# Relative attention takes in the norm ahead of it and the projection, norm and gate behind it

## The reference, cut to what matters

```
x = x + attn_a(layernorm(x))      # 16 heads of 16, relative positions in 63 buckets
x = x + ffn(layernorm(x))         # 16 experts, 512 tokens each, and a shared one
x = x + attn_b(layernorm(x))      # 16 heads of 64, window 128
x = x + ffn(layernorm(x))

def attn_a(x):                    # per batch b, head h
    q, k, v = split(x @ w_qkv.T); q = q * scale
    attn = q @ k.T + take(q @ rpe_k_table, idx) + take((k * scale) @ rpe_q_table, idx).T
    attn = softmax(attn)
    out = attn @ v + segment_sum(attn, buckets) @ rpe_v_table
    return heads_joined(out) @ w_proj.T + b_proj

def ffn(x):                       # its gate works on the normed rows
    scores = softmax(x @ gate_w.T)
    ...
```

## Time and profile before

| | us |
|---|---|
| median of 3 runs | 3925.07 |
| profiled execution | 3910.7 |
| its span | 3908.9 |
| first norm stage, from the span's start | 0 to 50.44 |
| relative stage's opening | 50.44 to 126.38 |
| its 32 units | 126.38 to 1156.86 |
| its last products and stores | 1156.86 to 1170.38 |
| second norm stage | 1170.38 to 1296.93 |
| the rest | 1296.93 to 3908.9 |

### The profile page before, as it was taken

How to read it: one execution, slowest core, us unless ns; L and a number is a source line. 1 busy time by engine, 2 the same in 40 slices (tenths; PEclk the granted TensorE clock), 3 DMA queues, 4 the chain that set the end, 5 groups by cost and what they waited for, 6 DMA issues and landing times. The chain is left out here.

```text
span 3908.9 us, 92834 instructions
## 1 busy us (share of the span) xinstructions
PE 3506.8 (90%) x33008; PEld 2695.1 (69%) x33008; DVE 2466.3 (63%) x5459; ACT 1826.1 (47%) x3736; POOL 1036.2 (27%) x1016
## 2 busy tenths in 40 slices
PE   3899999999986786999995999999999795999998
PEld 3566666666655675888884677667667585888887
DVE  5566666666664567676663666666666566666664
ACT  2566666666651323444442555455445432444443
POOL 0122222222220002333331343334333201232332
PEclk9999999999998897999998999999999897999999
DMA  5565666566545323443432000000000122443441
GB/s 189 151 171 167 173 174 173 167 175 175 168 129 180 115 74 126 117 119 109 116 92 82 13 20 18 21 21 18 18 21 19 59 81 100 124 113 103 127 114 32
DMA packets 372911, 407.00 MB, mean 104 GB/s; under 512 B 172689, under 2 KB 314385, under 8 KB 359057
## 3 DMA queue, kind: packets, MB, share of 16 engines
q1 hardware_dynamic: 347922, 368.09, 29.9%
q0 software_dynamic: 24576, 33.57, 4.9%
HBM read 255.49 MB, written 146.08 MB: 103 GB/s over the span
## 5 line engine op out<-in xcount | busy, mean ns | idle before, releaser
L2445 POOL TENSOR_TENSOR a_below<-a_probT,a_upper 128x512 f32<-128x512 f32 x128 | 164.3, 1283 | 724.6 <-ACT a_probT L2369 378.1
L2393 ACT ACTIVATE a_prob<-a_ps_s,a_low 128x512 f32<-128x512 f32 x512 | 319.2, 689 | 48.1 <-DVE a_low L2585 48.1
L1669 POOL TENSOR_TENSOR b_prob<-b_prob,b_rinv 128x512 f32<-128x512 f32 (+1 forms) x256 | 238.3, 935 | 386.5 <-DVE b_rinv L1730 386.3
L2254 PE MATMUL a_ps_p<-a_ident,a_prob 128*128 128x128 f32 x2048 | 309.3, 284 | 13.9 <-ACT a_band L2373 9.0
L2585 DVE TENSOR_REDUCE a_low<-a_ps_s 128x2 f32<-128x1024 f32 x256 | 313.5, 1225 | 8.8
L1607 ACT ACTIVATE b_prob<-b_score,b_low 128x256 f32<-128x256 f32 (+1 forms) x512 | 241.7, 474 | 129.6 <-DVE b_low L1725 113.8
L2254 PEld LDWEIGHTS a_ps_p<-a_ident,a_prob 128*128 128x128 f32 x2048 | 216.4, 141 | 106.1 <-issue 80.6
L2369 ACT COPY a_probT<-a_ps_p 128x512 f32<-128x512 f32 x352 | 193.9, 588 | 154.4 <-PE a_ps_p L2254 154.4
L1725 DVE CUSTOM_DVE_ANT_0 b_score<-b_ps_s,b_bias 128x256 f32<-128x256 f32 (+1 forms) x512 | 178.1, 385 | 74.9 <-PE b_ps_s L1548 71.6
L2584 DVE TENSOR_TENSOR a_ps_s<-a_ps_s,a_win 128x320 f32<-128x320 f32 (+1 forms) x256 | 135.0, 528 | 142.9 <-PE a_ps_s L2287 138.4
L903 POOL DMA_INDIRECT x<-fe_eo,fe_index_scatter x64 | 121.6, 1899 | 361.5 <-DVE fe_eo L1098 346.9
(11 more groups left out here) (426 smaller groups left out, 10402.1 us busy)
## 6 DMA issues: line engine op xcount, KB each, us to landing
a_win<-band SPq DMA_DIRECT2D x128, 384.0 KB, 4.8
prob<-a_prob SPq DMA_DIRECT2D x128, 384.0 KB, 3.6
shift<-a_gbias SPq DMA_DIRECT2D x64, 256.0 KB, 2.1
a_shifted<-shift SPq DMA_DIRECT2D x256, 64.0 KB, 2.0
a_bins<-prob SPq DMA_DIRECT2D x128, 128.0 KB, 3.5
fe_gT<-in_WgT SPq DMA_DIRECT2D x16, 1024.0 KB, 4.9
fe_uT<-in_WuT SPq DMA_DIRECT2D x16, 1024.0 KB, 5.2
fe_dT<-in_WdT SPq DMA_DIRECT2D x16, 1024.0 KB, 4.8
```

What stands on the lines that cost most here:

```text
L1669: nc.gpsimd.tensor_tensor(part, part, by_row, ALU.mult).then_inc(divided, 1)
L2254: last = nc.tensor.transpose(bank[:, c * P:(c + 1) * P], prob[:, t % 2, h, 32 + c * P:32 + (c + 1) * P], ident[:, :])
L2393: nc.scalar.activation(prob[:, t % 2, h, 32:32 + T], ps_s[pair][:, r, :], ACT.Exp, bias=low[:, h:h + 1]).then_inc(exped, 1)
L2445: nc.gpsimd.tensor_tensor(below[:, t % 2, :, :], probT[:, t % 2, :, t * P:(t + 1) * P], upper[:, :].unsqueeze(1).to_broadcast([P, HG, P]), ...
```

## The change

`norm_stage` is gone, and with it both of its uses. Its work is done inside the relative stage, for one batch at a time, in steps of the units:

- Batch b + 1, ahead: its x is loaded in round 0 (`xi`), its statistics are taken at the end of round 0, it is normalised in place in round 1 and transposed through `ps_w` (x_T) straight into `xT`. The split of x into two parts follows in the same round. For batch 0 this is done in the opening, with `ps_s` as bank.
- Batch b - 1, behind: the heads' results stay in the tile `o`, now of all 16 heads; in round 0 x is loaded again (`x1`) and GpSimd adds the bias; in round 1 heads are transposed (o_T); in round 2 they are multiplied by the projection in two halves (y), added into `x1`, and the norm is taken; in round 3 the normed rows `yn` (the same tile as `xi`) are transposed (y_T), stored both ways, and the gate's logits and softmax are made. For the last batch all of it follows after the units.

All new matmuls go through `ps_w`: LEAD and WHOLE have five new kinds, nine sections per batch. Not changed are the stages behind.

```diff
-LEAD = {"q": 3, "k": 3, "v": 2, "g_pos": 2, "g_low": 2, "g_up": 2, "s_pos": 1, "s_neg": 1, "band": 1, "bins_T": -1, "bins": -1, "out": -1}
+LEAD = {"q": 3, "k": 3, "v": 2, "g_pos": 2, "g_low": 2, "g_up": 2, "s_pos": 1, "s_neg": 1, "band": 1, "bins_T": -1, "bins": -1, "out": -1,
+        "x_T": 3, "o_T": -5, "y": -6, "y_T": -7, "logits": -7}
+WHOLE = ("q", "v", "k", "g_pos", "g_low", "g_up", "s_neg", "s_pos", "bins", "x_T", "o_T", "y", "y_T", "logits")
+ROUND_AT = {"x": 1, "in_stats": 0, "in_norm": 1, "in_pow": 0, "x_T": 1, "with_bias": 0, "o_T": 1, "y": 2, "y_stats": 2, "y_pow": 2, "y_norm": 2,
+            "y_T": 3, "logits": 3, "gate_exp": 3, "gate_end": 3}
...
-    ("max", 0), ("max", 1), ("s_pos", 0), ("probs_T", 3), ("s_neg", 0),
+    ("max", 0), ("max", 1), ("in_norm", 0), ("y", 0), ("s_pos", 0), ("probs_T", 3), ("s_neg", 0),
...
-        o = s.sb("o", [P, 2, NT, HG, AD])
+        o = s.sb("o", [P, NT, C])
+        xi = s.sb("xi", [P, NT, C])
+        x1 = s.sb("x1", [P, NT, C])
+        yn = xi
+        o_turned = s.sb("o_turned", [P, KC, T])
...
+                hold(sp, yn_out, 16 * b - 16, held)
+                hold(sp, ynT_out, 16 * b - 16, held)
+                sp.dma_start(xi[:, :, :], by_token(x_d, b)).then_inc(xi_in, 16)
+
+            def load_again(b):
+
+                hold(sp, x1_out, 16 * b + 16, held)
+                hold(sp, yn_ready, b + 1, held)
+                sp.dma_start(x1[:, :, :], by_token(x_d, b)).then_inc(x1_in, 16)
+
+            def store_x1(b):
+                hold(sp, emptied, section(b, 0, "y", 1) + 1, held)
+                sp.dma_start(by_token(x1_d, b), x1[:, :, :]).then_inc(x1_out, 16)
+
+            def store_normed(b):
+                hold(sp, yn_ready, b + 2, held)
+                sp.dma_start(by_token(xn_d, b), yn[:, :, :]).then_inc(yn_out, 16)
+
+            def store_turned(b):
+                hold(sp, emptied, section(b, 0, "y_T", 1) + 1, held)
+                sp.dma_start(by_channel(xnT_d, b), ynT[:, :, :]).then_inc(ynT_out, 16)
...
+                if has_step(b, g, "with_bias", 0):
+                    load_again(b - 1)
...
-                if g == 0 and not (isinstance(b, int) and b == B - 1):
-
-                    hold(sp, emptied, section(b, 2, "v") + 1, held)
+                if has_step(b, g, "in_stats", 0):
                     load_x(b + 1)
-                if has_step(b, g, "out", 0):
-                    store(*unit_before(b, g, 1))
+                if has_step(b, g, "y_norm", 0):
+                    store_x1(b - 1)
+                if has_step(b, g, "logits", 0):
+                    store_normed(b - 1)
                 home(b, g, 3)
+                if has_step(b, g, "logits", 0):
+                    store_turned(b - 1)
                 if has_step(b, g, "g_up", 0):
                     bias_out(*unit_after(b, g, 2), 0)
...
+            pe.wait_ge(in_normed, 1)
+            for c in range(KC):
+                for t in range(NT):
+                    last = nc.tensor.transpose(ps_s[0][:, c, t * P:(t + 1) * P], xi[:, t, c * P:(c + 1) * P], ident[:, :])
+            last.then_inc(first_turned, 1)
...
+                elif kind == "x_T":
+                    pe.wait_ge(in_normed, b + 1)
+                    for t in range(NT):
+                        last = nc.tensor.transpose(ps_w[:, t * P:(t + 1) * P], xi[:, t, k * P:(k + 1) * P], ident[:, :])
+                elif kind == "o_T":
+                    wait_copied(pe, b, NG - 1, "out", range(1))
+                    for t in range(NT):
+                        last = nc.tensor.transpose(ps_w[:, t * P:(t + 1) * P], o[:, t, k * P:(k + 1) * P], ident[:, :])
+                elif kind == "y":
+                    if b == 0 and k == 0:
+                        pe.wait_ge(late_in, 16 * 3)
+                    for t in (2 * k, 2 * k + 1):
+                        for c in range(KC):
+                            last = nc.tensor.matmul(ps_w[:, t % 2 * C:(t % 2 + 1) * C], o_turned[:, c, t * P:(t + 1) * P], proj[:, c, :],
+                                                    start=(c == 0), stop=(c == KC - 1))
+                elif kind == "y_T":
+                    pe.wait_ge(yn_ready, b + 2)
+                    for t in range(NT):
+                        last = nc.tensor.transpose(ps_w[:, t * P:(t + 1) * P], yn[:, t, k * P:(k + 1) * P], ident[:, :])
+                elif kind == "logits":
+                    for t in range(NT):
+                        for c in range(KC):
+                            last = nc.tensor.matmul(ps_w[:, t * E:(t + 1) * E], ynT[:, c, t * P:(t + 1) * P], gwT[:, c, :],
+                                                    start=(c == 0), stop=(c == KC - 1))
...
+                if kind == "x_T":
+                    last = nc.scalar.copy(xT[:, k, :], ps_w[:, :])
+                elif kind == "o_T":
+                    act.wait_ge(ynT_out, 16 * b + 16)
+                    last = nc.scalar.copy(o_turned[:, k, :], ps_w[:, :])
+                elif kind == "y_T":
+                    act.wait_ge(ynT_out, 16 * b + 16)
+                    last = nc.scalar.copy(ynT[:, k, :], ps_w[:, :])
...
+            def gate_exp(b):
+                act.wait_ge(emptied, section(b, 0, "logits") + 1)
+                nc.scalar.activation(sm[:, :, :], sm[:, :, :], ACT.Exp).then_inc(gate_exped, 1)
...
+                    if t == 3 and has_step(b, g, "in_pow", 0):
+                        power("in", b + 1)
+                    if t in (1, 2) and has_step(b, g, "with_bias", 0):
+                        with_bias(b - 1, t - 1)
+                    if t == 1 and has_step(b, g, "y_pow", 0):
+                        power("y", b - 1)
...
+            def with_bias(b, h):
+
+                hold(pool, x1_in, 16 * b + 16, held)
+                if isinstance(b, int) and b == 0 and h == 0:
+                    hold(pool, late_in, 16 * 3, held)
+                half = x1[:, 2 * h:2 * h + 2, :]
+                nc.gpsimd.tensor_tensor(half, half, bias[:, :].unsqueeze(1).to_broadcast([P, 2, C]), ALU.add).then_inc(biased, 1)
...
+            def moments_of(end, rows, b):
+                for t in range(NT):
+                    nc.vector.bn_stats(stats[end][:, t, :], rows[:, t, :]).then_inc(moments[end], 1)
+                hold(dve, moments[end], 2 * NT * b + NT, held)
+                for t in range(NT):
+                    nc.vector.bn_aggr(mv[end][:, t, :], stats[end][:, t, :]).then_inc(moments[end], 1)
+                hold(dve, moments[end], 2 * NT * b + 2 * NT, held)
+                nc.vector.tensor_scalar(var[end][:, :, :], mv[end][:, :, 1:2], LN_EPS, None, ALU.add).then_inc(var_ready[end], 1)
+
+            def normed(end, to, rows, b, ready):
+                hold(dve, rstd_ready[end], b + 1, held)
+                for t in range(NT):
+                    last = nc.vector.tensor_scalar(to[:, t, :], rows[:, t, :], mv[end][:, t, 0:1], rstd[end][:, t, :], ALU.subtract, ALU.mult)
...
+            def y_stats(b):
+                dve.wait_ge(emptied, section(b, 0, "y", 1) + 1)
+                moments_of("y", x1, b)
+
+            def y_norm(b):
+
+                hold(dve, yn_out, 16 * b + 16, held)
+                normed("y", yn, x1, b, yn_ready)
+
...
+                if kind == "y":
+                    dve.wait_ge(biased, 2 * b + k + 1)
+                    dve.wait_ge(filled, n + 1)
+                    half = x1[:, 2 * k:2 * k + 2, :]
+                    last = nc.vector.tensor_tensor(half, ps_w[:, :].rearrange("p (t c) -> p t c", c=C), half, ALU.add)
+                elif kind == "logits":
+                    logits = ps_w[:, 0:NT * E].rearrange("p (t e) -> p t e", e=E)
+                    dve.wait_ge(filled, n + 1)
+                    nc.vector.reduce_max(mx[:, :, :], logits, AX.X).then_inc(gate_step, 1)
+                    dve.wait_ge(gate_step, b + 1)
+                    last = nc.vector.tensor_tensor(sm[:, :, :], logits, mx[:, :, :].to_broadcast([P, NT, E]), ALU.subtract)
...
+            for k in range(2):
+                empty("y", B - 1, 0, ch, k)
+            y_stats(B - 1)
+            y_norm(B - 1)
+            empty("logits", B - 1, 0, ch)
+            gate_end(B - 1)
...
-        norm_stage(nc, "n0", ident, ins["x"], xnT)
-        relative_stage(nc, "a", ins, xnT, (ins["a_wT"], ins["a_wv"]), ins["a_rows"], ins["a_table"], ins["a_base"],
-                       ins["a_bins"], ins["a_bins_base"], ins["a_vbase"], trips, heads)
-        norm_stage(nc, "n1", ident, ins["x"], xnT, attn=(heads, ins["a_projT"], ins["a_bias"]), x1_d=x1, xn_d=xn, gate=ins["gateT"], scores=scores)
+        relative_stage(nc, "a", ins, ins["x"], (ins["a_wT"], ins["a_wv"]), ins["a_rows"], ins["a_table"], ins["a_base"],
+                       ins["a_bins"], ins["a_bins_base"], ins["a_vbase"], trips,
+                       ins["a_projT"], ins["a_bias"], ins["gateT"], x1, xn, xnT, scores)
```

(30 more changed lines are left out.)

404 lines of the change are left out of this document (110 added, 294 removed).

## The result

The changed kernel takes 3859.71 us (median of 4 runs, 3848.84 to 3863.76) against 3923.16 (3919.52 to 3925.45) for the kernel before on the same chip: ratio 0.9835, 95% interval [0.9812, 0.9857], 63 us faster. Two further sets of five runs gave 3858.58 (0.9822 [0.9802, 0.9842]) and 3855.02 (0.9827 [0.9813, 0.9840]). The forecast was 3863.

The account below looks back on a forecast made before the run. TensorE bounds the units, no engine the norm stages: 151.7 us saved at opening and end, less 89.9 of added work and waits, net 61.8 off the 3925.1 median, gives 3863 us, range 3820 to 3903.

Parts of the forecast that it names:

- The end: Last head result to next stage's first DMA: 129.7 us shrink to 24 (22 to 26), saving 105.7 us.
- The opening: Up to the first scores: first norm stage's 49.7 us go, less x's load and transposes; 46.0 us saved (44 to 48).
- The period: Each full batch in the units, 130.0 us before, costs 13.85 us more: added TensorE work plus waits.
- TensorE's work: Per full batch in the units: six transpose fills 2.94, y 3.56, logits 1.85; 8.35 us, nothing covering it.
- Waits: Per full batch in the units, four terms of delay brought by the new work: 5.5 us, of 3 to 13.
- Term (1): Round 2, tile 2: y's statistics between v and the maximum push bins, making q 2.15 us late (0.5 to 3).
- term (2): Round 1, tile 2: x's split between maxima and bins costs 1.8 us with the pair at 2.15; 0.9 at 1.29.
- the short waits: Heads' first transpose behind k's activations, s_pos behind x's normalisation, logits behind q's activation: 0.35 each, 1.05 us.
- DMA: Five 512 KB transfers a batch, x's reload in round 0 ahead of the shifted rows: 0.5 us (0 to 3).
- Rival A: In the units TensorE only looks full, so added work and waits vanish: 3773 us; chance 0.05.
- B: Nine sections per batch in the one bank ps_w each cost a full evacuation: 3918 us, no change; chance 0.09.
- C: SyncE's queue exposes each of five 512 KB transfers, 21.5 us a batch: slower, 4013 us; chance 0.06.

Follow-up runs that it names:

- The fillers: Changed kernel plus matmuls whose result nobody reads: ahead of the first q, 3853.52 us; also behind each section of the prologue, 3847.77 us.
- all five edits: Changed kernel with y's statistics ahead of v, logits behind scores, x split by halves, later reload, unread matmuls in the prologue: 3817.41 us, again 3816.62.
- The halves: Changed kernel with ScalarE and VectorE splitting x one half of the channels at a time, the first half earlier: 3852.41 us, ratio 0.9822.
- the half contraction: Changed kernel with y and logits computed from the first half of the channels alone, copies, waits and transfers kept: 3832.59 us, ratio 0.9769.
- the loop: Kernel with all five edits, TensorE's units of batches 1 to 6 as a loop instead of written out: 3876.82 us, ratio 0.9892.

## Why the prediction was right, and where not

**The end (-105.7): right.** 24.5 us from the last head result to the next stage's first DMA, forecast 24, and 24.5 to 24.7 in the two repeats.

**The opening (-46.0): wrong, and by the forecast's own test** (more than 3 us less than said). The failed step is "From 82.70 to the first scores at 126.38 the instructions are the same". They are, and up to the fold's taking at 36.71 the forecast held. But how long the same instructions take depends on the clock. Before, it rose at 90.4 and was low for only some 7 us after that; in the changed kernel it was low until 70 and again for some 7. Saved: 37.7 in this profile, 35.6 and 43.5 in the repeats. The fillers show that the clock is the cause. Why it rose early before and late after is not shown: TensorE stood just as long ahead of the first q (4.54 and 4.47 us), and the same program takes 42.0 to 51.8 us there from run to run.

**The period (+13.85): the sum right to 0.1 us, the terms not.** The waits named for rounds 1 and 2 are there, in the chains that the forecast described. Measured, per batch:

- TensorE's work, forecast 8.35. In the kernel with all five edits the clock is 1.00 and TensorE is busy 812.00 / 6 = 135.3 against 127.3: 8.0. Right within 0.35, and paid almost in full: 7.0 us in that kernel's quiet batches.
- Waits, forecast 5.5. TensorE's idle time grew by 3.5. Term (1) was 1.9 instead of 2.15; q's wait in round 1, term (2), 1.0 where 0.19 was before, 0.8 more instead of 1.8; the short waits 0.43 (logits), 0.26 (heads behind k) and none for s_pos; DMA at most 0.9, by a difference that the edit need not have made. The four terms' bounds add up to 1.0 to 10.3, not to the 3 to 13 that stand in the forecast; 3.5 lies in both.
- The low clock, not in the forecast: 10.4 of busy time less 8.0 of work is 2.4 us a batch, 1.0 of it behind term (1)'s wait and the rest mostly behind the logits.

Waits 2.0 too many, work 0.35 too much and clock 2.4 too little cancelled: the 0.1 us is luck. The failed step within the period is a term put at nothing, the clock behind a wait of a full TensorE. The range held because it took in both.

**Term (2).** The pair of splits took 1.28 us in its new place, not the 2.15 I chose. In the kernel before it ran from 565.53 beside a mask of GpSimd; here no mask runs (the nearest end at 563.39 and start at 570.59). GpSimd before, then VectorE after:

```profile
565.25 1.28 POOL L2445 TENSOR_TENSOR a_below<-a_probT,a_upper 128x512 f32<-128x512 f32 x1 [2.36 <-DVE a_probT L2568]
```

```profile
567.97 1.28 DVE L161 TENSOR_TENSOR a_x_rest<-a_xT,a_x_high 128x512 fp32r<-128x512 f32 x2
```

The halves show the same in one kernel: 1.04 beside a mask, 0.68 alone. That is what the Trainium skill (SBUF — State Buffer, "Who interferes with whom") says, and I should have priced by it: what stood beside an instruction belongs to its row as much as its length. Here its 0.9 would have been right (0.8 measured).

**Rival A** came from the Trainium skill (Perfetto Trace Analysis, "Identifying the Most-Contended Engine"). Weight loads stay 63% busy (545.81 of 863.74), and yet a quiet batch with all five edits is 7.0 us longer than before for 8.0 of added work; so in this stream of fp32 matmuls the rows decide, not the rule. **B** falls in size: only q, the logits and heads wait for the bank, 3.6 us a batch in all. Its mechanism is there under y's matmuls, as the half contraction shows. **C** falls with the period: VectorE waits 4.2 us in six batches for shifted rows and 2.1 for windows, where C has 21.5 a batch.

**The total, 3863 against 3860, is closer than the parts.** On the profiled pair the forecast is 15 us too good (61.8 against 47.0), of which 8.3 is the opening, 1.4 and 2.5 the first and the last batch. Adding 14 us for the profiled execution's distance from the median hid this: that the total is off by 4 is in part luck. The later stages took 2612.0 us in before's profile and 2605.9 to 2616.5 (mean 2612.0) in the twelve after the change without the loop. So the 12 us by which that profile lies below its median are probably not there but in the first 1297 us. Its stretch from the first q to the first scores, 39.3 us, is shorter than all eight of the changed prologue without fillers. If that was luck, the 46.0 was nearer to the mean saving than 37.7 is; with one profile of before this stays open.

## What to carry to other kernels

Look for the slack of a step's own engine before placing it: y's statistics cost 3.1 us a batch after v and nothing ahead of it, where VectorE stood 2.1 us for v. Price a wait of a full TensorE together with the clock behind it: 1.9 us of standing cost 3.1 on average. When an experiment hits its number, look whether its rounds moved where the theory said: half a contraction less met 2.8 us with 1.4 of work and 1.6 of clock. And in a sparse prologue the clock is part of the sum: instructions that are the same don't take the same time.

## What the hardware showed that I had not expected

- A wait of 1.9 us in a stream that was else full was followed by some 3 us at 1.2 GHz in four of six batches, and 0.43 us ahead of 1.96 us of 16-column matmuls by the same in five of six; 1.96 us of them without the wait was not, nor was the wait with half of them.
- Matmuls for nobody made the prologue 10 us shorter (37.4 in four profiles instead of 47.9 on average in eight) although TensorE did more.
- A loop's turn on TensorE cost 5 to 6 us in two waits, most of them called issue, where the written-out program had one wait of 0.6 to 2.6 us now and then.
